# A graph network kernel: its opening reordered, with differences taken on VectorE and weights in homes of their own

## The reference, cut to what matters

```python
# layer 0
h = relu(bn1(conv1(xc)))                    # 1 tap, xc is x transposed
h = bn2(conv2(h))                           # 17 taps, padding 8
x_conv = relu(h + xc)
s = x @ w_se.T + b_se                       # 3 numbers a token
A = exp(-(|s_i|^2 + |s_j|^2 - 2 s_i.s_j))
x_nmp = A * adj  @  relu(x @ w_msg.T + b_msg)
y = gru_gates([x_conv, x_nmp], x)           # w_ih, w_hh: r, z, n
x = layernorm(x + y)
# layer 1
h = relu(((1 + eps) * x + adj @ x) @ W1 + b1)
x = layernorm(x + h @ W2 + b2)
```

## Time and profile before

| what | value |
| --- | --- |
| median of 3 runs | 388.86 us (388.27 to 390.04) |
| the profiled execution's own time | 390.09 us |
| its span in the trace | 388.3 us |
| PE busy | 363.9 us, 94% |
| DVE busy | 327.9 us, 84% |
| ACT busy | 231.5 us, 60% |
| POOL busy | 223.3 us, 58% |
| chain that ended last | PE 60%, DVE 30%, issue 5%, DMA 2% |

### The profile page before, as it was taken

How to read it: one execution, slowest core, us unless ns; L and a number is a source line. 1 busy time by engine, 2 the same in 40 slices (tenths; PEclk the granted TensorE clock), 3 DMA queues, 4 the chain that set the end, 5 groups by cost and what they waited for, 6 DMA issues and landing times.

```text
span 388.3 us, 6417 instructions
## 1 busy us (share of the span) xinstructions
PE 363.9 (94%) x2150; PEld 314.4 (81%) x2150; DVE 327.9 (84%) x669; ACT 231.5 (60%) x435; POOL 223.3 (58%) x195
## 2 busy tenths in 40 slices
PE   4969998899999999999999999999999999999974
PEld 1747866798888998989888898989888898988953
DVE  3999999999699986999689986999789986977564
ACT  4455345563866566673775667674676558472773
POOL 3346173698428763597437863597537863395342
PEclk9998998999999999999999999999999999999998
DMA  6500003130110210120100300130101201000011
GB/s 231 223 0 3 0 0 114 51 111 1 56 54 18 93 43 13 56 108 0 54 23 31 108 27 27 54 108 0 57 5 50 110 2 54 3 0 2 0 56 54
DMA packets 7991, 19.39 MB, mean 50 GB/s; under 512 B 672, under 2 KB 5024, under 8 KB 6944
## 3 DMA queue, kind: packets, MB, share of 16 engines
q1 hardware_dynamic: 7536, 18.50, 13.6%
q10 hardware_dynamic: 432, 0.59, 0.4%
HBM read 14.90 MB, written 4.19 MB: 49 GB/s over the span
## 4 chain that ended last, share of the span: by engine, by line
PE 60%; DVE 30%; issue 5%; DMA 2%; ACT 1%; POOL 1%; SPq 0%; DVEq 0%; ACTq 0%
PE back L1222 25%; PE conv L1222 17%; PE back L1335 6%; PE back L1424 3%; DVE stats L991 3%; DVE stl L821 3%; DVE tail L1025 2%; PE front L1307 2%; DMA tail<-in_conv_dram 2%; DVE nmpl L821 2%; DVE adjT L1087 2%; DVE wl L1044 2%; PE back L1386 2%; DVE sv L842 1%; PE front L1327 1%
## 5 line engine op out<-in xcount | busy, mean ns | idle before, releaser
L1222 PE MATMUL conv<-sth,wh 128*128 128x256 f32 x217 | 65.4, 301 | 2.0 <-DVE stl L821 1.9
L1222 PE MATMUL conv<-stl,wh 128*128 128x256 f32 x217 | 61.8, 285 | 0.0
L1222 PE MATMUL conv<-sth,wl 128*128 128x256 f32 x217 | 61.7, 284 | 0.0
L524 POOL TENSOR_TENSOR rstd<-rstd,minus_half 128x4 f32<-128x4 f32 (+1 forms) x34 | 38.7, 1138 | 34.0 <-DVE rstd L995 33.4
L542 POOL TENSOR_TENSOR amat<-amat,adjT 128x512 f32<-128x512 f32 x32 | 50.4, 1604 | 4.6 <-ACT amat L663 4.6
L529 POOL TENSOR_TENSOR xw<-xw,xv 128x512 f32<-128x512 f32 (+1 forms) x17 | 21.4, 1256 | 50.0 <-ACT xw L687 50.0
L1222 PEld LDWEIGHTS conv<-sth,wh 128*128 128x128 f32 x217 | 40.9, 189 | 4.7 <-DVE stl L821 1.8
L1222 PEld LDWEIGHTS conv<-stl,wh 128*128 128x128 f32 x217 | 41.0, 189 | 0.1
L1222 PEld LDWEIGHTS conv<-sth,wl 128*128 128x128 f32 x217 | 40.8, 188 | 0.0
L619 ACT ACTIVATE sth<-sv 128x272 fp32r<-128x272 f32 (+1 forms) x33 | 17.3, 523 | 33.6 <-DVE sv L842 21.5
L536 POOL TENSOR_TENSOR tail<-xn,later_w 128x512 f32<-128x512 f32 (+1 forms) x17 | 30.8, 1815 | 4.3 <-DMA out_dram<-tail 2.6
(11 more groups left out here) (225 smaller groups left out, 1028.1 us busy)
## 6 DMA issues: line engine op xcount, KB each, us to landing
adjT<-in_adj_dram SPq DMA_DIRECT2D x8, 1024.0 KB, 4.8
out_dram<-tail SPq DMA_DIRECT2D x15, 256.0 KB, 2.2
xv<-in_x_dram SPq DMA_DIRECT2D x7, 512.0 KB, 3.3
gbuf<-in_gates_dram SPq DMA_DIRECT2D x1, 576.0 KB, 6.5
tail<-in_conv_dram ACTq DMA_DIRECT2D x2, 256.0 KB, 3.7
xv<-in_x_dram SPq DMA_DIRECT2D x2, 256.0 KB, 5.0
later_w<-in_later_dram SPq DMA_DIRECT2D x1, 452.0 KB, 7.2
tail<-in_conv_dram SPq DMA_DIRECT2D x1, 320.0 KB, 5.3
```

The costliest lines, as they stand in the source:

```text
L524: done(pool.tensor_tensor(rstd[:, k, h, q], rstd[:, k, h, q], minus_half[:, q], ALU.pow), RSTD[k])
L1222: ins = pe.matmul(bank, a, b, start=first and k == 0, stop=last and k == len(todo) - 1)
```

## The change

SyncE no longer issues the second half of group 0's x before the convolution's weights; ScalarE issues it behind its own two pieces of those weights, in the place of the identity matrix, which SyncE now issues behind group 1's x. SyncE waits only for the halves of x before it loads group 1's.

On VectorE, the low part of x's second half comes after the three sums of HALF, both differences of group 0 and of group 1 are VectorE's, as are the streams of PLUS1 and MINUS1 of group 0; `factors` stands ahead of `parts1`. ScalarE makes `diag`. GpSimd keeps the two streams of point 2, the masks, the diagonals (from another place) and the low parts of group 1's x, which move into the first pass. The weights of HALF and PLUS2 lie in a larger `first_w`, so their high and low parts can be taken last. TensorE takes all four distances ahead of PLUS1.

```diff
-        first_w = sb("first_w", [P, NVEC + P])
+        first_w = sb("first_w", [P, NVEC + 10 * P])
...
+        small = sb("small", [P, 15 + BLK + len(SCALES)])
...
-        W_ORDER = ("conv1", "gates", HALF, PLUS2, PLUS1, ZERO, MINUS2, MINUS1, INF, "w1")
+        W_ORDER = ("conv1", "gates", PLUS1, MINUS2, ZERO, MINUS1, INF, "w1", HALF, PLUS2)
...
# SyncE, prologue
-                done(sp.dma_start(xv[0][:, cols(1)], x_v[0, :, cols(1)]), X_LOADED)
...
-                sp.wait_ge(conv2_loaded, 64)
                 wait(sp, X_LOADED, 0, 16)
                 load_x(1, 1)
+                sp.dma_start(ident, t["consts"]).then_inc(consts_loaded, 16)
# GpSimd, prologue
-                pool.wait_ge(pads_zeroed, 2)
-                token_diffs(0, 1)
                 streams2(0)
-                streams1(0)
-                token_diffs(1)
                 for b in range(GB):
                     mask(0, 0, b)
                 streams2(1)
-                pool.wait_ge(bn_ready, 4)
-                for b in range(GB):
-                    add_diagonal(0, 0, b)
-                for h in range(PAIRS):
...
+                pool.wait_ge(diag_ready, 1)
+                wait(pool, NH_READY, 0, 1)
+                add_diagonal(0, 0, 0)
+                add_diagonal(0, 0, 1)
+                wait(pool, MSUM_READY, 1, 1)
+                add_diagonal(0, 0, 2)
+                add_diagonal(0, 0, 3)
# GpSimd, steady
                 residual(gb, 1 - u, 0)
+                if first:
+                    wait(pool, U_READY, gm, 1)
+                    x_low1(0)
                 residual(gb, 1 - u, 1)
                 rsqrt(0, gb, 0)
+                if first:
+                    x_low1(1)
                 rsqrt(0, gb, 1)
# ScalarE, prologue
-                act.dma_start(ident, t["consts"]).then_inc(consts_loaded, 16)
+                done(act.dma_start(xv[0][:, cols(1)], x_v[0, :, cols(1)]), X_LOADED)
...
-                act.wait_ge(tap_sums, 6)
-                tap_high(HALF)
-                h1_out(1, 0, True)
-                h1_out(1, 1, True)
-                act.wait_ge(bn_ready, 3)
-                factors_out(0)
-                minus2_out(0)
-                tap_high(PLUS2)
+                act.wait_ge(consts_loaded, 16)
+                act.wait_ge(eps_ready, 1)
+                act.activation(diag[:, :], ident, ACT.Copy, scale=eps1[:, 0:1]).then_inc(diag_ready, 1)
+                factors_out(0)
+                h1_out(1, 0, True)
                 exps(0, 0)
                 exps(0, 1)
+                h1_out(1, 1, True)
+                exps(0, 2)
+                exps(0, 3)
+                act.wait_ge(bn_ready, 3)
+                minus2_out(0)
                 act.wait_ge(tap_sums, 11)
                 tap_high(PLUS1)
-                tap_high(ZERO)
-                exps(0, 2)
-                exps(0, 3)
                 minus1_out(0)
                 tap_high(MINUS2)
...
# VectorE, prologue
-                x_low(0, 0, 1)
+                dve.tensor_scalar(eps1[:, :], vec[:, EPS1:EPS1 + 1], 1.0, None, ALU.add).then_inc(eps_ready, 1)
...
+                taps_step(half, half, 0.5, w1)
+                taps_step(half, half, 0.5, w0)
+                x_low(0, 0, 1)
+                first_diffs(0)
...
+                taps_step(odd, w2, 4.0, w0)
+                taps_step(minus2, w3, 4.0, w1)
+                wait(dve, C1_FULL, 1, 2)
+                taps_step(plus2, minus2, 2.0, odd)
+                taps_step(minus2, minus2, -2.0, odd)
+                factors(0)
                 parts1(0)
-                factors(0)
+                first_streams1()
...
                 u_sum(0, 0)
+                pair2_sum(0)
+                first_diffs(1)
                 half_stream(1)
                 zero_stream(1)
-                pair2_sum(0)
+                parts2(1)
                 pair2_add(0)
-                parts2(1)
...
                 nmp_low(0, 0)
+                xconv_low(0, 0)
                 w_low_part(wl[:, S_GATE:S_GATE + 9, :], graw, wh[:, S_GATE:S_GATE + 9, :], w_count("gates"))
-                xconv_low(0, 0)
+                tap_low(PLUS1)
                 xconv_low(0, 1)
                 nmp_low(0, 1)
-                tap_low(HALF)
-                tap_low(PLUS2)
-                tap_low(PLUS1)
-                stream_low(1, 2)
-                dve.wait_ge(consts_loaded, 16)
-                dve.scalar_tensor_tensor(diag[:, :], ident, vec[:, EPS1:EPS1 + 1], ident,
-                                         ALU.mult, ALU.add).then_inc(bn_ready, 1)
# VectorE, steady, first pass only
                 parts1(gm)
                 if first:
-                    tap_low(ZERO)
-                    tap_low(MINUS2)
+                    stream_low(gm, 2)
                 gates(gb, 1 - u, 0)
                 if first:
-                    tap_low(MINUS1)
+                    tap_low(MINUS2)
                 gates_end(gb, 0)
                 stream_low(gm, 3)
+                if first:
+                    tap_low(ZERO)
+                    tap_low(MINUS1)
...
                 pair1_add(gm, 1)
+                if first:
+                    tap_low(HALF)
+                    tap_low(PLUS2)
                 out_stats(gb, 0)
# TensorE, prologue
                 factors(0)
-                distances(0, 0)
-                distances(0, 1)
+                for b in range(GB):
+                    distances(0, b)
                 plain_taps(0, PLUS1)
-                distances(0, 2)
-                distances(0, 3)
                 plain_taps(0, MINUS1)
```

More of the change, by code:

```diff
@@ L128, in gnn_kernel @@
         b2bc = later_w[:, W2_AT + 2 * D + P:W2_AT + 2 * D + 2 * P]
[L129 to L135, removed]
+        small = sb("small", [P, 15 + BLK + len(SCALES)])
+        rs, one, three, eps1 = small[:, 0:2], small[:, 2:3], small[:, 3:4], small[:, 4:5]
+        bn, gbias, minus_half = small[:, 5:11], small[:, 11:15], small[:, 15:15 + BLK]
+        sc = small[:, 15 + BLK:]
         diag = sb("diag", [P, P])
@@ L308, in gnn_kernel @@
         later_loaded = sem("later_loaded")
+        eps_ready = sem("eps_ready")
+        diag_ready = sem("diag_ready")
         exponent_set = sem("exponent_set")
@@ L458, in prologue @@
             def prologue():
-                sp.dma_start(first_w[:, :], t["first"]).then_inc(first_loaded, 16)
+                sp.dma_start(first_w[:, 0:NVEC + P], t["first"]).then_inc(first_loaded, 16)
                 sp.dma_start(xv[0][:, cols(0)], x_v[0, :, cols(0)]).then_inc(x_pair0_loaded, 16)
-                done(sp.dma_start(xv[0][:, cols(1)], x_v[0, :, cols(1)]), X_LOADED)
                 sp.dma_start(c2raw[:, 0:5, :], t["conv2"][:, 0:5, :]).then_inc(conv2_loaded, 16)
@@ L543, in mask, with x_low1 @@
                      A_READY)
+            def x_low1(h):
+                wait(pool, XH_READY, 1, h + 1)
+                done(pool.tensor_tensor(xl[1][:, cols(h)], xv[1][:, cols(h)], full(xh[1][:, cols(h)]), ALU.subtract),
+                     XL_READY)
             def add_diagonal(g, u, b):
@@ L583, in steady @@
                 streams1(gm)
+                first = isinstance(s, int) and s == 1
                 residual(gb, 1 - u, 0)
+                if first:
+                    wait(pool, U_READY, gm, 1)
+                    x_low1(0)
                 residual(gb, 1 - u, 1)
                 rsqrt(0, gb, 0)
+                if first:
+                    x_low1(1)
                 rsqrt(0, gb, 1)
@@ L761, in prologue @@
                 stream_high(1, 2)
+                tap_high(INF)
+                act.activation(w1h[:, :], w1raw, ACT.Copy).then_inc(w_high, 1)
+                tap_high(HALF)
+                tap_high(PLUS2)
             def steady(s, u, front):
@@ L831, in stream_low, with first_diffs, first_streams1 @@
                 low(rows(stl, j), rows(sv, j), rows(sth, j), LS_READY)
-            def first_diffs():
-                wait(dve, H1_READY, 0, 2)
+            def first_diffs(g):
+                wait(dve, H1_READY, g, 2)
+                wait(dve, RI_READY, g - 1, 1)
                 done(dve.tensor_tensor(av[:, 0:2, :, :].rearrange("p r b t -> p b r t"), h1[:, :, :, 1, :],
                                        h1[:, :, :, 0, :], ALU.subtract), A_DIFF)
+                done(dve.tensor_tensor(av[:, 2:4, :, :].rearrange("p r b t -> p b r t"), one_on(h1[:, :, :, 0, :]),
+                                       h1[:, :, :, 1, :], ALU.subtract), A_DIFF)
+            def first_streams1():
+                wait(dve, PV_READY, 0, 1)
+                r = ROW[PLUS1]
+                done(dve.tensor_tensor(sv[:, r, :, :], vv[:, 1, :, :], vv[:, 0, :, :], ALU.add), R1_READY)
+                done(dve.tensor_tensor(sv[:, r + 1, :, :], vv[:, 1, :, :], vv[:, 0, :, :], ALU.subtract), R1_READY)
             def half_stream(g):
@@ L1087, in taps_step @@
                     dve.scalar_tensor_tensor(out, a, scale, b, ALU.mult, ALU.add).then_inc(tap_sums, 1)
```

(11 more changed lines are left out.)

41 lines of the change are left out of this document (17 added, 24 removed).

## The result

| | before | changed |
| --- | --- | --- |
| median of 7 runs | 389.28 us (388.27 to 390.04) | 386.98 us (386.80 to 388.15) |
| ratio | | 0.9949, 95% interval 0.9935 to 0.9964 |
| profiled execution, its span | 390.09, 388.3 us | 386.80, 385.0 us |

The changed kernel is faster by 2.0 us by the ratio (1.4 to 2.5) and by 2.3 us by the medians. The sum had said 3.5. The profiled pair differs by 3.3 us, close to that sum; but this flatters it, since the profiled execution of before was a long one and that of after a short one. A second execution of each, profiled beside the experiments, had spans of 387.2 and 386.5 us. The four together are the ground of what follows.

A forecast was written before the change was run, and what follows sets the result against it. The prediction took VectorE to bound the opening, 85.7 us of its program deciding when TensorE's dense part begins. Terms +3.2, -7.0, -1.5, +1.6, +0.4, -0.2 sum to -3.5 us: median 388.86 to 385.4, range 382.4 to 388.4.

The forecast's parts named there:

- its own sign: VectorE's chain from first sum of weights to TensorE's dense stretch should be about 82 us, else the forecast fails.
- Waits that go: VectorE's opening: waits for GpSimd vanish at HALF's last sum, both groups' `factors` and two sums, -7.0 us.
- Added: VectorE's opening: differences, two streams and a low part of x come, the diagonal leaves; +3.2 us.
- Masks: GpSimd's four masks beside VectorE: fall mostly beside PSUM readers, then meet group 1's differences; -1.5 us.
- GpSimd instead: GpSimd's moved diagonals, low parts of x, and work near HALF's and PLUS2's low parts slow VectorE; +1.6 us.
- New wait: VectorE at `pair2_sum`, waiting for ScalarE's `minus2_out`; 0 to 2 us, taken as +0.4 us.
- Start: Weights land sooner with half of x moved to ScalarE's queue, sharing bandwidth; -0.2 us.
- TensorE's 9.0 us of loss: TensorE's idle and low-clock time in the opening, 9.0 us, covers the gain; first gates reached about 3 us sooner.
- (b): Rival, chance 0.13: TensorE's clock drops at PLUS1 anyway, costing 1.75 us; gates' products come late, VectorE waits; 387.1 us.
- (a): Rival, chance 0.14: GpSimd's moved work meets only PSUM readers and `pair2_sum` doesn't wait; -6.6, 382.3 us.
- (c): Rival, chance 0.08: the lead is spent in the first pass, ahead of the stream TensorE needs; 388.9 us.
- (d): Rival, chance 0.09: GpSimd's moved operations still meet VectorE's SBUF readers, only a third of relief comes; +2.2, 391.1 us.

The follow-up runs named there:

- Differences only: Kernel before with only GpSimd's differences and group 0's PLUS1 and MINUS1 streams given to VectorE, in their old places; ratio to before 0.9962, -1.5 us.
- low parts of x only: Kernel before with only GpSimd's low parts of group 1's x moved into the first pass; ratio to before 0.9954, -1.8 us.
- h1 early: Changed kernel with both `h1_out` of group 1 moved ahead of `factors_out` on ScalarE; ratio to the kernel before 0.9951, -1.9 us.
- Nmp first: Changed kernel with PLUS1's low parts moved behind `nmp_low(0, 1)`; ratio to the kernel before 0.9922, -3.0 us, against 0.9948 for the changed kernel.
- the transfers alone: Kernel before with only SyncE's and ScalarE's new transfer orders; ratio to before 1.0018, +0.7 us.

## Why the prediction was right, and where it was off

The direction, the range (382.4 to 388.4) and the mechanism held: the opening was VectorE's, it waited for GpSimd's turns, and what it gained came through to the end. The size was 2.0 to 2.3 us instead of 3.5. That the time lies in the range says little, for the range is 6 us wide and reaches down to a gain of 0.9. The median, 386.98, is just outside the forecast's own 384.0 to 386.8 and above the 386.9 from which it called a gain measurable, though the interval of the ratio, 0.9935 to 0.9964, is clear of 1. By its own sign, a chain of about 82 us from the first sum to TensorE's stretch, the sum was too good: the chain was 85.7 and 85.5 us before, and 83.5 and 84.4 after.

- *Waits that go, -7.0.* Held to a tenth: 1.0, 1.9, 1.2 and 2.9 us in the rows of after. Differences only and low parts of x only show it as cause: 1.5 and 1.8 us, where their expectations had 1.2 and at most 2.
- *Added, +3.2.* 3.0 by the starts of the same rows.
- *Masks, -1.5.* The term held: the two differences of group 1 take from 30.50 to 33.09, 2.6 us for 1.3, so 1.3 over; 1.1 was taken.
- *GpSimd instead, +1.6.* The two adds beside the diagonals take 2.30 us for 1.3; 1.0 was taken. HALF's and PLUS2's low parts were mis-sized: 2.69 us for 1.55, so 1.1 and not 0.3, two differences of GpSimd beside them. What the sum didn't have evens this out: the two adds just ahead of them take 2.37 us, and took 3.46 before.
- *New wait, +0.4.* 0.46 us in one execution and 1.57 in the other, where x's second half landed late, which the prediction had held to be hidden. But h1 early removed the wait and gave nothing, for the masks behind it bind; as a term of its own it was nearly nought, and the masks' term holds it. In the execution with 1.57 it cost some 0.6 us, an estimate: its masks end at 33.38, and the half stream begins at 34.63.
- *Start, -0.2.* The means of the 14 traces differ by 0.2. The 1.1 us of the profiled pair is scatter. By the rule of the Trainium skill (DMA: Bandwidth & Descriptors, Queues, rings and completion order) that each transfer engine takes turns between queues, 0.2 was due, and by order of issue 0.7. The means are nearer to the rule, but a scatter of 1.5 us makes them weak evidence.

The step that failed is the sentence "TensorE's 9.0 us of loss cover this: it arrives at the first gates about 3 us sooner". This is its first matmul of the gates before, and in the changed kernel:

```profile
47.51 0.49 PE L1222 MATMUL back<-xh,wh 128*128 128x512 f32 x1
```

```profile
45.96 0.47 PE L1246 MATMUL back<-xh,wh 128*128 128x512 f32 x1
```

That is 1.5 us sooner, but the first sum was 1.1 sooner already. Counted from the first sum it is 38.3 us before and 37.8 after, and 38.4 and 38.7 in the second executions: TensorE gained next to nothing up to there. With the differences only it takes 36.2. A part of the loss is seen. The new order puts PLUS1's low parts, 0.75 us, ahead of `nmp_low(0, 1)`, behind those of the gates' weights that stood there before (2.09 us for both), and `nmp_low(0, 1)` frees the bank of group 1's second messages. TensorE waits 0.85 us for it, then VectorE 0.48 us for the messages and 0.96 us for the gates. VectorE had neither wait before. That is 1.4 us on the chain that the sum, taken along VectorE alone, had no term for. Nmp first gets 1.0 of it back.

Of the rivals, (b) had the time nearest to the measured one, 387.1, and its second half came true: the gates' products reached VectorE late. But its cause, a drop of the clock at PLUS1, is not that. It comes and goes: the granted clock in 25 to 30 us was 0.72 in one profiled execution of the changed kernel and 1.00 in the other, and the ten matmuls took 3.83 and 2.44 us. The execution at full clock was the longer of the two (386.5 against 385.0 us of span), and TensorE stopped for `nmp_low` in both. (a), (c) and (d) didn't come true.

What stays open: that x's late half is what the transfers alone cost the kernel before (0.7 us) is seen in one trace only, and of the reordering only the place of `nmp_low(0, 1)` and of `h1_out` was tried by itself.

## What to carry to other kernels

Where VectorE bounds a stretch and GpSimd works on SBUF beside it, price GpSimd's help by what it adds to VectorE's rows, from a stretch in which it is idle: engines that meet only through semaphores in the program met here in SBUF as well. Moving it beside PSUM readers, or giving its work back to VectorE, can both be gains. A sum along the bounding engine needs a second look at what the others get from it late: an operation that frees a bank is worth more than one whose result is wanted only in the next pass. And one trace of each kernel can be 1 us off where starts scatter by as much; count from a common event in the trace, or take a second one.

## What was not expected

- The first sum of weights began anywhere from 7.76 to 9.30 us in 14 profiled executions, and up to 1.3 us apart (7.76 to 9.06) in the seven of them with the changed kernel's transfers and the changed kernel's work of VectorE ahead of it.
- A wait can be taken away at no gain although it stands on the chain: behind VectorE's 0.46 us before `pair2_sum` stood the four masks, and without it the differences beside them took as much longer.
- A lower granted clock of TensorE need not lengthen the run when VectorE bounds, though VectorE may meet it. With the low parts of x put back, the windows from 65 to 75 us show 0.55 and 0.76, behind a wait of TensorE of 3.5 us, where the changed kernel had 1.00 in both. TensorE's products with the adjacency came late, and VectorE waited 1.01 us for ScalarE, which waited for them. Yet messages of group 2 came just 1.2 us later than in the changed kernel. VectorE had got that wait back: GpSimd's differences were late too, and two adds and two low parts, 2.37 and 2.69 us in the changed kernel, took 1.28 and 1.55 without them. What the clock alone costs was not tried.

```profile
65.00:70.00 5.00, 3.14 (x15) 3.17 (x16) 4.56 (x13) 2.38 (x6) 2.25 (x2) 0.55 0.03 12
70.00:75.00 5.00, 5.00 (x24) 4.16 (x23) 3.79 (x9) 2.59 (x5) 4.76 (x4) 0.76 0.00 0
```

```profile
74.72 0.69 DVE L826 TENSOR_TENSOR nmpl<-back,nmph 128x512 fp32r<-128x512 f32 x1 [1.01 <-ACT nmph L622]
```
